# Four chained cross-attention blocks on one core: the second layer's context keys and values are computed at the end of the first joined stage, and one layer norm goes ahead of weight casts

## The chip, the cores and the metric

One Trainium2 chip, one of its cores. The metric is the device time of one launch in microseconds (us). Engines by the names of the profile: PE (TensorE matmul; PEld is its weight load), DVE (VectorE), ACT (ScalarE), POOL (GpSimd), SP (SyncE, which issues all DMAs here).

## The reference, cut to what matters

Tokens x are 2 x 1024 x 256 (B = 2, T = 1024, D = 256); the context is 2 x 77 x 256. Four blocks follow each other. The first two matter here.

```python
# block L0: causal self-attention over the tokens and the context, 16 heads of 16
qkv = _ln(x, g1, be1) @ w_qkv + b_qkv
ckv = context @ w_ckv + b_ckv
k, v = concat([k_self, k_ctx]), concat([v_self, v_ctx])
x = x + softmax(mask(q k^T / 4)) v
hdn = gelu(_ln(_ln(x, g2, be2), gf, bf) @ w1 + b1)        # exact gelu, 1024 wide
x = x + (hdn @ w2 + b2)
# block L1: three layers, 4 heads of 64; the first one attends from the tokens to the context
K = relu(context @ Wk[0] + bk[0]); V = relu(context @ Wv[0] + bv[0])
Q = relu(x @ Wq[0] + bq[0]); out = softmax(Q K^T / 8) V * query_mask + x ; ...
```

K and V of layer 0 of L1 depend on the context and weights alone, not on x. Blocks L2 (cross-attention by token index) and L3 (attention to the context and a feed-forward) are not touched.

## The kernel before, in words

The program is a row of stages. `next_stage` ends each: every engine drains and adds one to a semaphore, and all wait until all five have. POOL then clears the semaphores of the stage that is over. In a stage each engine runs a list of its own, in the order in which it is written; semaphores tie the lists.

**Stage 1, the joined front** (`front_tensor`, `front_scalar`, `front_vector`, `front_gpsimd`, `front_sync`). Normalised tokens are turned, and 18 feature items (L570: queries and keys of L0, 128 features by 512 tokens, split into three bf16 parts by ACT L607 and L588, DVE L642 and POOL L682) alternate with 18 value items (L576, DVE L637). Each item is stored to HBM by SP (L697, L700). The number of a place in this list counts both kinds (0 to 35). From number 24 on, the row maxima of head group 0 run between the items. A maximum is a chunk: PE multiplies into bank 6 or 7 (L1218), DVE reduces it (L1446 or L1450). There are 43 chunks, 7 for context keys and 9 for each of 4 heads. 19 of them and the final M (a transpose of the maxima, L1223, and its split into three bf16 rows, L1465 to L1474) come after the last item. SP loads group 1's stack between the stores (`NEXT_STACK_AT`), and at the end sends the three rows (L1074).

**Stage 2, attention of L0** (`attention_tensor` and others). Eight groups; scores L1251, exponentials ACT L1411, causal triangles POOL L1188, products with values L1276. POOL's list begins with `context_prepare_gpsimd` (L1125, L2065): it clears KBD, the block-diagonal keys of L1's first layer, and writes REP, the context features repeated for four heads. SP loads the feed-forward's weights and L1's first weights and rows in `load_more`.

**Stage 3, feed-forward of L0** (`first_ffn_*`, `ffn_*`). Float weights and tokens are split into a high part and a remainder. Tokens are in four chunks of 512. The list of each engine begins:

- PE: `context_tensor` (L2073 keys, L2082 and L2084 values, six sets of two products and a bias), then the transposes of chunk 0 (L1686), then hidden tiles (L1618, six matmuls each) and, three tiles later, the second product (L1633).
- ACT: high parts of the first half of the weights, roots, chunk 0's normalisation (L1711), `context_keys_scalar` (L2094), `context_values_scalar` (L2102), then chunk 0's two feature tiles (L1678) and their high parts (L1595).
- DVE: moments of chunk 2 (L1767 to L1699), scalings (L1704, L1706), four casts of the second half of the weights (L1786), the scaling of chunk 2, `attention_moments` of chunk 3, the two token remainders of chunk 0 (L1600), without which no hidden tile starts.
- POOL: `split_low` (L1588), four remainders of each half of the weights; then `context_gpsimd` (L2110, L2112), which blanks the foreign heads of the values.

```python
        e.wait_ge(sp.w_high, 1)                       # before, first_ffn_vector
        for i in range(4, 8):
            h = e.tensor_copy(W_H[:, a], W0_FF[:, a])
        scaling(e, n2, 2)
        attention_moments(e, n2, 3)
        for k in range(KT):
            split_tokens_vector(e, s, 0, k)
```

## Time and profile before

| | us |
|---|---|
| three runs | 1535.41, 1539.99, 1544.95 (median 1539.99) |
| the profiled execution, its own time | 1534.61 |
| its span | 1532.9 |
| PE busy | 1328.7 (87%) |
| DVE busy | 1068.3 (70%) |
| ACT busy | 739.0 (48%) |
| POOL busy | 538.3 (35%) |
| stage 1 | about 14 to 93 |
| stage 2 | about 93 to 397.2 |
| stage 3 | from 397.2 |

A busy PE in these rows is not PE at its peak: its matmuls count as busy at either clock, and at the lower one they take longer. PEclk is the granted clock as a share of full speed: 1.00 is 2.4 GHz, 0.50 is 1.2 GHz. The chain of waits is the list of what ended last at each moment; work that is not on it has slack.

### The profile page before, as it was taken

The page shows a single profiled execution, that of the slowest core. Times are in us where ns is not written, and L with a number is a line of the kernel's source. Part 1 is how long each engine was busy: PE and PEld are TensorE (multiplying, and loading weights), DVE is VectorE, ACT ScalarE, POOL GpSimd, SP SyncE. Part 2 cuts the span into 40 slices and gives each one's busy share as a digit, 9 for nine tenths or more (in the row PEclk, how much of TensorE's full clock was granted, in tenths as well). Part 3 has the DMA queues.
Part 4 walks back from the last instruction along what each step waited for, and adds up shares of the span by engine and source line. Part 5 has one row for each costly group of instructions (what it writes and reads, how often), then busy time and mean ns, then how long its engine had stood idle before and what let it go on. Part 6 is the DMA issues. An engine that isn't in the chain of part 4 may idle for free.

```text
span 1532.9 us, 21753 instructions
## 1 busy us (share of the span) xinstructions
PE 1328.7 (87%) x7242; PEld 766.8 (50%) x7242; DVE 1068.3 (70%) x2667; ACT 739.0 (48%) x1030; POOL 538.3 (35%) x462
## 2 busy tenths in 40 slices
PE   7879999998699879879999989799998789688897
PEld 4423333332388656644443356344444577445796
DVE  6668888885654377767566867676777888676654
ACT  4335665667675346423334445233444644344664
POOL 3311111112410053216876622267864356001212
PEclk9969999999899998979999999799999889899998
DMA  6974333300000001562440217704400020630001
GB/s 202 265 197 95 59 59 59 59 2 2 28 1 1 1 1 69 174 177 48 97 97 26 91 52 215 187 15 97 97 28 28 8 29 32 157 66 2 1 1 55
DMA packets 80021, 110.39 MB, mean 72 GB/s; under 512 B 16712, under 2 KB 55810, under 8 KB 78118
## 3 DMA queue, kind: packets, MB, share of 16 engines
q1 hardware_dynamic: 79910, 109.00, 28.5%
q8 instruction: 58, 0.95, 0.3%
q14 instruction: 53, 0.43, 0.1%
HBM read 70.62 MB, written 37.83 MB: 71 GB/s over the span
## 4 chain that ended last, share of the span: by engine, by line
PE 40%; POOLq 19%; DVE 16%; issue 11%; ACT 6%; DVEq 3%; DMA 2%; SPq 1%; POOL 1%; ACTq 0%
POOLq L1165 19%; PE banks L1276 6%; PE banks L1618 5%; PE banks L1633 5%; PE banks L1218 4%; PE banks L2204 3%; PE banks L1251 3%; PE banks L2234 2%; DVE max_parts L1450 1%; DVE mask_rows L1446 1%; PE banks L1229 1%; ACT x_feat L1411 1%; DVE max_parts L1435 1%; PE banks L2222 1%; DVE scratch L1446 1%
## 5 line engine op out<-in xcount | busy, mean ns | idle before, releaser
L1411 ACT ACTIVATE x_feat<-banks,key_bias 128x1024 f32<-128x1024 f32 x160 | 176.4, 1113 | 263.3 <-PE banks L1258 207.1
L1164 POOL TENSOR_TENSOR x_feat<-x_feat 128x1024 f32<-128x1024 f32 (+1 forms) x112 | 243.0, 2170 | 94.4 <-ACT x_feat L1411 85.9
L1218 PE MATMUL banks<-stacks 128*128 128x512 f32 (+4 forms) x640 | 224.2, 399 | 37.1 <-DVE max_parts L1439 12.4
L1276 PE MATMUL banks<-x_feat,v_group 128*32 128x512 f32 (+4 forms) x1312 | 231.6, 569 | 8.4 <-ACT x_feat L1411 4.8
L1411 ACT ACTIVATE x_feat<-banks 128x1024 f32<-128x1024 f32 (+2 forms) x224 | 178.8, 841 | 112.0 <-PE banks L1251 110.9
L1218 PEld LDWEIGHTS banks<-stacks 96*128 96x128 bf16 (+1 forms) x640 | 78.8, 138 | 219.5 <-DVE max_parts L1439 91.8
L1251 PE MATMUL banks<-stacks 99*128 99x512 bf16 (+3 forms) x512 | 129.8, 344 | 18.7 <-ACT x_feat L1411 13.0
L1188 POOL TENSOR_SCALAR_AFFINE_SELECT x_feat<-x_feat 128x256 f32<-128x256 f32 x128 | 53.4, 420 | 244.1 <-ACT x_feat L1411 242.4
L1439 DVE CUSTOM_DVE_ANT_0 scratch<-banks,mask_rows 128x512 f32<-128x512 f32 x128 | 88.2, 689 | 49.8 <-PE banks L1218 49.7
L1257 PE MATMUL banks<-stacks 128*128 128x512 f32 x256 | 110.9, 433 | 9.5 <-DMA stacks<-neg_max_parts_r 9.5
L1618 PE MATMUL banks<-stacks 128*128 128x512 f32 x384 | 102.0, 405 | 9.8 <-DVE stacks L1600 8.9
L1258 PE MATMUL banks<-stacks 96*128 96x512 f32 x256 | 103.2, 403 | 0.0
L1633 PE MATMUL banks<-stacks 128*128 128x256 f32 x768 | 102.9, 286 | 0.0
L1633 PEld LDWEIGHTS banks<-stacks 128*128 128x128 f32 x768 | 99.9, 193 | 3.9
L1450 DVE TENSOR_REDUCE max_parts<-banks 128x1 f32<-128x512 f32 x128 | 84.3, 687 | 13.2 <-PE banks L1218 12.5
L1439 DVE CUSTOM_DVE_ANT_0 w_even<-banks,mask_rows 128x512 f32<-128x512 f32 x112 | 77.0, 688 | 10.8 <-PE banks L1218 10.7
L1618 PEld LDWEIGHTS banks<-stacks 128*128 128x128 f32 x384 | 70.6, 195 | 23.1 <-issue 9.6
L2204 PE MATMUL banks<-x_feat,w_odd 128*128 128x512 f32 x160 | 80.5, 632 | 0.8 <-ACT x_feat L2323 0.8
L1276 PEld LDWEIGHTS banks<-x_feat,v_group 128*32 128x32 f32 (+1 forms) x1312 | 41.5, 119 | 78.5 <-issue 53.1
L1257 PEld LDWEIGHTS banks<-stacks 128*128 128x128 f32 x256 | 49.5, 193 | 60.2 <-issue 42.6
L1251 PEld LDWEIGHTS banks<-stacks 99*128 99x128 bf16 x512 | 44.7, 99 | 56.3 <-ACT x_feat L1411 29.9
L1435 DVE TENSOR_REDUCE max_parts<-banks 128x5 f32<-128x385 f32 (+2 forms) x104 | 53.7, 546 | 27.1 <-PE banks L1207 13.6
(308 smaller groups left out, 2457.4 us busy)
## 6 DMA issues: line engine op xcount, KB each, us to landing
stacks<-q_parts_r SPq DMA_DIRECT2D x18, 512.0 KB, 6.9
stacks<-k_parts_r SPq DMA_DIRECT2D x18, 512.0 KB, 10.5
q_parts_r<-stacks SPq DMA_DIRECT2D x16, 512.0 KB, 3.2
k_parts_r<-stacks SPq DMA_DIRECT2D x16, 512.0 KB, 3.1
v_group<-v SPq DMA_DIRECT2D x14, 512.0 KB, 14.7
stacks<-q_parts SPq DMA_DIRECT2D x16, 384.0 KB, 5.0
stacks<-q_parts SPq DMA_DIRECT2D x16, 256.0 KB, 7.6
w_even<-in_w SPq DMA_DIRECT2D x4, 1024.0 KB, 14.4
```

The costliest lines, as they stand in the source:

```text
L1164: e.tensor_tensor(total, total, p, ALU.add)
L1165: e.drain().then_inc(s.tile_summed, 1)
L1218: m = e.matmul(PS[:, bank, at:at + wide], q[0:rows, h, qt * P:(qt + 1) * P], keys[0:rows, h, k0:k0 + wide], start=True, stop=True, skip_gr ...
L1251: m = e.matmul(o, k[0:rows, head_of_k(A, r, h), k0:k0 + P], q[0:rows, h, qs], start=True, stop=True, skip_group_check=True)
L1257: e.matmul(o, ka[:, hk, ks], qa[:, h, qs], start=True, stop=False)
L1258: m = e.matmul(o, kb[0:96, hk, ks], qb[0:96, h, qs], start=False, stop=True)
L1276: m = e.matmul(PS[w * h:w * (h + 1), bank, t.q0:CH], V[:, h, :], PB[:, t.index % 2, h // 2, h % 2, 0:CH - t.q0], start=t.first, stop=t.las ...
L1411: e.activation(dst, PS[:, 2 * (st % 2):2 * (st % 2) + 2, 0:CH - t.q0], ACT.Exp, scale=A.scale, bias=bias).then_inc(s.p_ready, 1)
L1439: e.tensor_tensor_reduce(scratch, PS[:, bank, :], MB[:, k0:k0 + CH], 1.0, LOWEST, ALU.add, ALU.max, maxp[:, h, qt, half:half + 1]).then_in ...
L1618: mm = e.matmul(PS[:, i % 3, :], w[:, k, ms], x[:, c % 2, k, :], start=k == 0 and w is w1h and x is XH, stop=k == KT - 1 and w is w1l)
L1633: mm = e.matmul(o, h[:, i % 4, ts], w[:, m, :], start=m == 0 and t % 2 == 0 and h is HID_H and w is w2h, stop=m == MT_F - 1 and h is HID_L ...
L2204: m = e.matmul(PS[:, n % 2, :], left, right, start=k == 0, stop=k == KT - 1)
```

## The change

L1's context keys and values leave stages 2 and 3 and go to the end of stage 1. REP is written by POOL ahead of feature item 11 (and lies at another place of the same buffer), KBD is cleared by POOL after the last item. Two weight loads and a row of biases leave `load_more` and go into SP's list after number 22. PE's list at the end of stage 1 first waits until all remainders and values are taken, then runs the 19 chunks with the key products behind chunk 32 and three value sets behind chunks 35, 37 and 39; the other three sets come behind M. ACT's bias and relu and POOL's blanking come at the end of their stage 1 lists, so the barrier waits for them. In stage 3 DVE's four casts go behind chunk 3's moments and chunk 0's token remainders.

```diff
+        for n in "qf":                                   # load_more
+            e.dma_start(W1[0][n], kp(a["W" + n][0])).then_inc(ld.w1a, 16)
-        load_layer(e, 0, ld.w1a)
...
+    REPEAT_AT = 11
+    KEYS_BEHIND, VALUES_BEHIND = 11, {8: (0, 0), 6: (0, 1), 4: (0, 2)}
...
+        need(e, s.left, len(items[0]))                   # front_tensor
+        e.wait_ge(stored0.v_taken, len(items[1]))
         for x in front_maxima(A, len(items[0]), 0):
             attention_chunk(e, A, *x, 0, -1)
+            if x[0] == "A" and len(A.chunks) - x[2] == KEYS_BEHIND:
+                context_keys_tensor(e, cx)
+            if x[0] == "A" and len(A.chunks) - x[2] in VALUES_BEHIND:
+                context_values_tensor(e, cx, *VALUES_BEHIND[len(A.chunks) - x[2]])
+        for j in range(3):
+            context_values_tensor(e, cx, 1, j)
...
+        context_keys_scalar(e, cx)                       # front_scalar, after the last item
+        context_values_scalar(e, cx)
...
+            if i == REPEAT_AT:                           # front_gpsimd
+                e.wait_ge(tn.taken, KT * 3)
+                context_repeat_gpsimd(e)
...
+        e.wait_ge(stored0.v_taken, len(items[1]))
+        e.wait_ge(s.product, len(items[0]))
+        fill(e, KBD, 0.0)
+        e.drain().then_inc(cx.cleared, 1)
+        context_gpsimd(e, cx)
...
+            if number == CONTEXT_WEIGHTS_AT:             # front_sync, 22
+                load_context_weights(e)
...
-        context_tensor(e, cs)                            # first_ffn_tensor
...
-        e.wait_ge(cs.keys_ready, 1)
-        e.wait_ge(cs.values_ready, B)
...
-        context_keys_scalar(e, cs)                       # first_ffn_scalar
-        context_values_scalar(e, cs)
...
+        scaling(e, n2, 2)                                # first_ffn_vector
+        attention_moments(e, n2, 3)
+        for k in range(KT):
+            split_tokens_vector(e, s, 0, k)
         e.wait_ge(sp.w_high, 1)
         for i in range(4, 8):
             a = slice(CH * i, CH * (i + 1))
             h = e.tensor_copy(W_H[:, a], W0_FF[:, a])
         h.then_inc(sp.w_high, 1)
-        scaling(e, n2, 2)
-        attention_moments(e, n2, 3)
-        for k in range(KT):
-            split_tokens_vector(e, s, 0, k)
```

**The first place is PE at the end of stage 1.** Before, from the ninth chunk of head 2 to the second group's first chunk:

```order
L1218 MATMUL banks<-stacks 128x256 x2
L1218 MATMUL banks<-stacks 128x512 x6
L1218 MATMUL banks<-stacks 128x128
L1218 MATMUL banks<-stacks 128x384
L1218 MATMUL banks<-stacks 128x128
L1218 MATMUL banks<-stacks 128x384
L1218 MATMUL banks<-stacks 128x256 x2
L1223 MATMUL banks<-ident,max_rows 32x128
L1251 MATMUL banks<-stacks 128x512 x2
L1207 MATMUL banks<-stacks 128x77 x5
```

Now, from the keys (L2103; w_odd holds Wk and Wv) on. L1254 is the former L1218, L2115 and L2117 are a value set and its bias:

```order
L2103 MATMUL banks<-ctx_feat,w_odd 128x154 x4
L1254 MATMUL banks<-stacks 128x256 x2
L1254 MATMUL banks<-stacks 128x512 x2
L2115 MATMUL banks<-w_odd,w_even 103x128 x2
L2117 MATMUL banks<-rows_odd,ones_row 103x128
L1254 MATMUL banks<-stacks 128x512 x2
L2115 MATMUL banks<-w_odd,w_even 103x128 x2
L2117 MATMUL banks<-rows_odd,ones_row 103x128
L1254 MATMUL banks<-stacks 128x512 x2
L2115 MATMUL banks<-w_odd,w_even 103x128 x2
L2117 MATMUL banks<-rows_odd,ones_row 103x128
```

The keys stand ahead of the last chunk of head 2, the value sets between the chunks of head 3. The rest of the piece, up to the barrier:

```order
L1254 MATMUL banks<-stacks 128x256 x2
L1259 MATMUL banks<-ident,max_rows 32x128
L2115 MATMUL banks<-w_odd,w_even 103x128 x2
L2117 MATMUL banks<-rows_odd,ones_row 103x128
L2115 MATMUL banks<-w_odd,w_even 103x128 x2
L2117 MATMUL banks<-rows_odd,ones_row 103x128
L2115 MATMUL banks<-w_odd,w_even 103x128 x2
L2117 MATMUL banks<-rows_odd,ones_row 103x128
```

Three sets now stand between M and the barrier.

**The second place is DVE at the start of stage 3.** Before, from the second of the first two scalings:

```order
L1706 SCALAR_TENSOR_TENSOR minus_mean_rstd<-mean_var,rstd 128x4
L1786 CAST stacks<-w_even 128x512 x4
L1704 RECIPROCAL rstd<-std 128x4
L1706 SCALAR_TENSOR_TENSOR minus_mean_rstd<-mean_var,rstd 128x4
L1767 TENSOR_TENSOR x_res<-x_res,y_tok 128x1024
L1691 BN_STATS stats<-x_res 128x6 x4
L1696 BN_AGGR mean_var<-stats 128x2 x4
L1699 TENSOR_SCALAR var_eps<-mean_var 128x4
L1600 TENSOR_TENSOR stacks<-x_feat,stacks 128x512 x2
```

Now, the same lines with new numbers:

```order
L1742 SCALAR_TENSOR_TENSOR minus_mean_rstd<-mean_var,rstd 128x4
L1740 RECIPROCAL rstd<-std 128x4
L1742 SCALAR_TENSOR_TENSOR minus_mean_rstd<-mean_var,rstd 128x4
L1798 TENSOR_TENSOR x_res<-x_res,y_tok 128x1024
L1727 BN_STATS stats<-x_res 128x6 x4
L1732 BN_AGGR mean_var<-stats 128x2 x4
L1735 TENSOR_SCALAR var_eps<-mean_var 128x4
L1636 TENSOR_TENSOR stacks<-x_feat,stacks 128x512 x2
L1821 CAST stacks<-w_even 128x512 x4
```

The casts moved behind the two token remainders.

## Rows read from the trace of the kernel before

**Rows 1.** the chain of waits, 70 to 105 us: start us, us, what

```profile
77.85 0.62 PE banks L1218
...
78.50 0.70 DVE max_parts L1450
...
89.00 0.39 PE banks L1223
...
92.29 1.84 DMA stacks<-neg_max_parts
...
94.27 1.02 PE banks L1251 x2
...
100.27 1.72 PE banks L1276 x8
```

**Rows 2.** timeline at full clock: start us, us, engine, line, operation

```profile
77.25 0.39 PE L1218 MATMUL banks<-stacks 96*128 96x512 bf16 x1 [0.21 <-DVE max_parts L1450]
...
133.24 0.60 PE L1251 MATMUL banks<-stacks 99*128 99x512 bf16 x2
```

**Rows 3.** PE by stretch of 1 us: busy (instructions), PEclk, DMA share, GB/s

```profile
75.00:76.00 1.00, 0.00 (x0) 1.00 1.07 329
...
84.00:85.00 1.00, 0.82 (x3) 0.50 0.80 299
...
101.00:102.00 1.00, 1.00 (x11) 0.65 1.19 216
...
408.00:409.00 1.00, 0.63 (x4) 0.95 0.00 0
...
419.00:420.00 1.00, 1.00 (x6) 0.93 0.00 0
```

**Rows 4.** timeline of the work that moves, on PE, ACT and POOL

```profile
95.49 1.34 POOL L2065 COPY w_even<-ctx_feat 128x616 f32<-128x616 f32 x2
...
397.30 1.32 PE L2073 MATMUL banks<-ctx_feat,w_odd 128*128 128x154 f32 x8 [0.89 <-DVEq L279]
...
404.00 0.46 PE L2084 MATMUL banks<-rows_odd,ones_row 1*103 1x128 f32 x2
...
404.78 1.56 ACT L2094 ACTIVATE w_even<-banks,cols 64x154 f32<-64x154 f32 x4
...
406.36 0.87 ACT L2102 ACTIVATE w_even<-banks 103x384 f32<-103x384 f32 x2
...
412.94 0.99 POOL L2110 TENSOR_SCALAR_AFFINE_SELECT w_even<-w_even 103x384 f32<-103x384 f32 x1
...
413.89 0.53 POOL L2112 TENSOR_SCALAR_AFFINE_SELECT w_even<-w_even 103x384 f32<-103x384 f32 x1
```

**Rows 5.** the chain of waits where the joined stage's values end

```profile
74.97 0.33 DVE v_group L637
```

**Rows 6.** timeline of SP: the group 1 values are issued

```profile
82.68 0.34 SPq L1015 DMA_DIRECT2D v_group<-v  x1
```

**Rows 7.** the chain of waits into the feed-forward stage, 385 to 430 us

```profile
404.32 2.08 DVE stacks L1786 x3
...
406.56 1.20 DVE minus_mean_rstd L1706
...
411.27 0.59 DVE stacks L1600
...
411.86 1.68 DVEq L1705
```

**Rows 8.** timeline of POOL, DVE and PE in the feed-forward stage

```profile
400.26 5.19 POOL L1588 TENSOR_TENSOR stacks<-w_even,stacks 128x512 fp32r<-128x512 f32 x4 [5.86 <-ACT stacks L1580]
...
406.48 6.50 POOL L1588 TENSOR_TENSOR stacks<-w_even,stacks 128x512 fp32r<-128x512 f32 x4 [1.03 <-DVE stacks L1786]
...
413.69 0.24 DVE L1706 SCALAR_TENSOR_TENSOR minus_mean_rstd<-mean_var,rstd 128x4 f32<-128x4 f32 x1
...
421.76 1.59 PE L1633 MATMUL banks<-stacks 128*128 128x256 f32 x12
```

More of the change, by code:

```diff
@@ L711, in program, with load_context_weights @@
     NEXT_STACK_AT, FIRST_VALUES_AT = (24, 27, 30), 32
+    CONTEXT_WEIGHTS_AT = 22
+    def load_context_weights(e):
+        for n in "kv":
+            e.dma_start(W1[0][n], kp(a["W" + n][0])).then_inc(cx.loaded, 16)
+        e.dma_start(RB[0:1, 0:1, :], a["rows1"][0:1, :].unsqueeze(0)).then_inc(cx.loaded, 16)
     def front_sync(e, items, A):
@@ L2046, in program @@
     NK = 4 * SC + 1
-    REP = WF[:, 640:640 + KT * B * NK].rearrange("p (k b n) -> p k b n", k=KT, b=B)
+    REP = WF[:, 3584:3584 + KT * B * NK].rearrange("p (k b n) -> p k b n", k=KT, b=B)
     VB = WF[:, 640:640 + 768].rearrange("p (b j n) -> p b j n", b=B, j=3)
@@ L2058, in program, with context_repeat_gpsimd @@
     LSTEPS = 4 * (NC + 2) + 2
-    def context_prepare_gpsimd(e):
-        fill(e, KBD, 0.0)
+    def context_repeat_gpsimd(e):
         fill(e, REP[:, :, :, 4 * SC:NK], 0.0)
@@ L2075, in context_tensor, with context_values_tensor @@
         mm.then_inc(s.key_product, 1)
+    def context_values_tensor(e, s, b, j):
         ones, bias = ONES_ROW[0:1, 0:KROWS], row(RB, ROWS_L1, "bv0")
-        for b in range(B):
-            for j in range(3):
-                cols = slice(64 * j, 64 * j + P)
-                o = PS[0:KROWS, 4 + b, j * P:(j + 1) * P]
-                for k in range(KT):
-                    e.matmul(o, REP[:, k, b, KROWS * j:KROWS * (j + 1)], W1[0]["v"][:, k, cols], start=k == 0, stop=False,
-                             skip_group_check=True)
-                mm = e.matmul(o, ones, bias[0:1, cols], start=False, stop=True, skip_group_check=True)
-        mm.then_inc(s.value_product, 1)
+        if (b, j) == (0, 0):
+            e.wait_ge(s.repeated, 1)
+        cols = slice(64 * j, 64 * j + P)
+        o = PS[0:KROWS, 4 + b, j * P:(j + 1) * P]
+        for k in range(KT):
+            e.matmul(o, REP[:, k, b, KROWS * j:KROWS * (j + 1)], W1[0]["v"][:, k, cols], start=k == 0, stop=False,
+                     skip_group_check=True)
+        mm = e.matmul(o, ones, bias[0:1, cols], start=False, stop=True, skip_group_check=True)
+        if (b, j) == (B - 1, 2):
+            mm.then_inc(s.value_product, 1)
     def context_keys_scalar(e, s):
         e.wait_ge(s.key_product, 1)
+        e.wait_ge(s.cleared, 1)
         for m in range(KT):
@@ L2093, in context_keys_scalar @@
                 at = COLS["L1k"] + m
-                last = e.activation(KBD[rows, m, :, SC * h:SC * (h + 1)],
+                e.activation(KBD[rows, m, :, SC * h:SC * (h + 1)],
                                     PS[rows, m, 0:B * SC].rearrange("p (b n) -> p b n", b=B), ACT.Relu, bias=COL[rows, at:at + 1])
-        last.then_inc(s.keys_ready, 1)
     def context_values_scalar(e, s):
@@ L3169, in _ @@
         e.wait_ge(ld.w1c, 32)
+        e.wait_ge(ld.w1a, 48)
         nxt()
```

32 lines of the change are left out of this document (17 added, 15 removed).

## The prediction, before the changed kernel ran

> **What bounds the kernel now.** I read the chain of waits first, because each of the changed places lies at a seam between two stages, where busy shares say little. At the end of stage 1 it alternates between a chunk on PE, 0.62 us, and its maximum on DVE, 0.70 us; after the transpose of the maxima it runs through the three row transfers, which land at 94.13, to PE's first scores at 94.27 [rows 1]. The timeline shows the same chunk in 0.39 us, and a pair of score products in 0.60 instead of 1.02, where the clock is full [rows 2]. So I read the granted clock next: PE did nothing from 75 to 76, and the clock was half while PE's records filled 0.8 of each microsecond; it was full again only within 101 to 102 [rows 3]. It fell again at 408.95, after PE had stood idle but for one set of transposes since 405.6, and came back at 419.07, 5.4 us after PE had begun to work without a gap [rows 3]. Last I read the timeline of the work that moves [rows 4] and the chain into the feed-forward [rows 7], where DVE and not the moved work is what ends last.
>
> **Stage 1, the added wait.** PE may start chunk 24 only when the last value is taken, at 75.30 [rows 5]; before, that chunk was ready and DVE took it at once. One chunk of 0.39 [rows 2] and some 0.25 of semaphores and fill are now waited for: +0.7. Behind the wait stand only the 19 chunks. Below it can't go much, as the wait is certain; above it could be 0.9, if the clock has already fallen.
>
> **Stage 1, the inserts.** The key products took 1.32 us; the six value sets filled 398.6 to 404.46, so 1.0 each, all at full clock [rows 4]. At half clock I stretch them by 1.6, the ratio of the chunk (0.62 to 0.39): 2.1 and 1.6. DVE needs 1.39 for two chunks, and at half clock PE's 0.62, DVE's 0.70 and 0.07 between them are 1.39 too [rows 1]: no slack, so an insert costs its length less 0.1, and the keys 0.2 less again, since the chunk ahead of them takes DVE longer. That is 1.8 + 3 x 1.5 = 6.3. At full clock the same circle takes 1.16, which leaves 0.23 ahead of time and 0.3 in the chunk behind: keys 0.6, sets 0.5, together 2.1. The upper bound is the doubling of the full-clock prices, 8.1.
>
> Between 2.1 and 6.3 the clock decides. Work at 0.8 of the records did not bring it back in eleven microseconds; work without a gap did, after 3.3 us up to 101.35 and after 5.4 us up to 419.07 [rows 3]. With the inserts PE has hardly a gap from the keys on. I take it that the clock comes back behind the first value set: 1.8 + 1.5 + 2 x 0.5 = 4.3. The Trainium skill (TensorE: Matmul & The Clock Gate, "What's actually happening") says that the array is throttled by default and that sustained activity releases it. By that rule the sum is the one with 4.3; by the rows from 78 to 88 alone, where a busy PE stayed slow, it is the one with 6.3.
>
> **Stage 1, the tail.** M's transpose ends at 89.39 [rows 1]. Behind it come three sets (3.0 at full clock, 4.8 at half), ACT's two activations (0.87), POOL's two blankings (0.99 and 0.53 beside DVE work; DVE is idle here, so 0.53 each) [rows 4], and 0.4 of semaphores and drains: PE could start at 94.7 or 96.5. It started at 94.27, for the rows landed then. So +0.4 or +2.2; with doubled sets +3.5. SP's loads of group 2 start as much later; nothing asks for them in the first tiles. The split of the maxima and the row transfers run beside this and are covered.
>
> **Stage 1, what is covered.** REP's two copies (1.34 [rows 4]) stand ahead of item 11 on POOL, which idled 34 us in this stage waiting for ACT; if that cover were gone, item 11's store would be 1.7 late, and its buffer is asked for by nobody after it. Two weight loads of 256 KB and a row enter SP's queue at about 54 us, ahead of the stores and of group 1's stack. At the 267 GB/s of those microseconds they cost the queue 2 us. The group 1 values are issued at 82.68, when all stores have landed [rows 6]; 2 us later is still ahead of 89, so 0. If a store's landing did hold a buffer, the whole 2 us would be paid.
>
> **Stage 2.** POOL's preparation at 94.5 to 96.8 [rows 4] was over before the first triangle at 99.9: its removal is worth 0. With the clock full at the start, the six PE pieces of the chain from 94.27 to 101.98 (the first 1.02, the last 1.72 [rows 1], 5.3 in all) shrink to 0.6 of it: -2.1. If the clock is half, 0.
>
> **Stage 3.** PE's context products (397.30 to 404.46) ended before the first transposes could start at 404.93: 0. ACT's six activations (1.56 + 0.87 [rows 4]) delayed chunk 0's feature tiles by 1.6, but DVE reached their remainders only at 411.19: off the path. What lies on it is DVE's list [rows 7]: the casts, 2.08, leave it. The scaling's 1.20 stays, since POOL still works on the first half until 405.45 [rows 8]. The second remainder shows 1.68 for a piece that should be about 0.7, beside POOL's second half (406.48 to 412.98 [rows 8]); now POOL waits for the casts at that time and is idle: -0.9. Together -3.0, and the first hidden tile starts at 410.7 instead of 413.68. ACT's high part of the second tile, freed of the six activations, is ready at 408.7, in time.
>
> The price is POOL's second half. It starts at 413.0, behind the casts (410.5 + 2.5), and takes 5.19 to 6.50 [rows 8]: it ends at 418.2 to 419.5. The second product, at 421.76 before [rows 8], now asks for it at 418.7. So the gain is 2.2 to 3.0; I take 3.0. A DVE operation on 4 columns took 1.20 beside POOL's subtraction [rows 7] and 0.24 once it was over [rows 8]. The Trainium skill (SBUF — State Buffer, "Who interferes with whom") says why: a VectorE instruction with two SBUF inputs and a GpSimd instruction that reads SBUF block each other whole. By that rule the first three remainders of the hidden tiles may each wait for one of POOL's four pieces, and these for them; the trace agrees with the rule, and what it can cost is rival 3.
>
> **The sum.** 0.7 + 4.3 + 0.4 - 2.1 - 3.0 = +0.3. The profiled execution took 1534.61, which is 5.4 under the median of the three runs; the forecast is 1534.9 for such an execution and 1540.3 for the median.
>
> **The rivals.**
> 1. *The clock stays at half to the end of stage 1.* For it: it did so for eleven microseconds before [rows 3], and the waiting for the last value makes the gap ahead longer. Against it: the inserts fill the gaps. 0.7 + 6.3 + 2.2 - 3.0 = +6.2, so 1546.2; slower than before. With all upper bounds 0.7 + 8.1 + 3.5 - 2.2 = +10.1. It decides if the granted clock is still 0.50 when M is transposed. 30%.
> 2. *The clock never falls, or is back with the keys.* 0.7 + 2.1 + 0.4 - 2.1 - 3.0 = -1.9, so 1538.1. For it only that PE's gaps are what let it fall, and the keys come 5 us after. 12%.
> 3. *The change doesn't do what it says in stage 3*: POOL's second half becomes the new end. If its four pieces and three DVE remainders of 0.7 take turns, it ends at 421.5, and nothing is gained there: 0.7 + 4.3 + 0.4 - 2.1 = +3.3, so 1543.3. 10%.
> 4. *The weights push a store past its buffer's turn*: +2 on the forecast, 1542.3. Against it: 7 us between the issue of the group 1 values and their use. 6%.
>
> **How the numbers follow.** The forecast has 42%. About 1%, 15 us, is what a measurement of this kernel can tell from no change, and no case reaches it. The three runs lie within 9.5 us, so half of that, 4.8, goes on either side: from 1538.1 - 4.8 = 1533 to 1546.2 + 4.8 = 1551, and one more for the upper bounds. Faster by over 1% 2%, within 1% 94%, slower by over 1% 4%, all for what no case has priced.
>
> **What would show it.** Right: DVE's idle time between 76 and the barrier grows by 4 to 6 us, with the clock back at 1.00 before M; the first scores some 5.5 us later than 94.27; stage 2 shorter by 2; from the barrier of stage 3 to the first hidden tile 13.4 us instead of 16.4, with the casts behind it. Wrong: a clock of 0.50 at the start of stage 2, a hidden tile that waits for ACT or for POOL, or a store that ACT waits for.

## The result and the profile after

| | kernel before | changed kernel |
|---|---|---|
| median of the runs (range) | 1536.54 us (1530.77 to 1544.95, 12) | 1541.01 us (1535.44 to 1552.2, 12) |
| ratio, 95% interval | | 1.0039 [1.0023, 1.0056] |
| profiled execution, own time / span | 1534.61 / 1532.9 | 1545.09 / 1543.3 |

The change makes the kernel slower by 0.39%: 6.0 us, between 3.5 and 8.6. The forecast was +0.3, which lies outside that interval. That the forecast time, 1540.3, lies 0.7 from the new median is mostly luck: the three runs that it started from had their median 3.5 above that of the twelve.

I read each stage as the time between the moments at which the last engine is through `next_stage` (us, one profiled execution each, one row for each kernel). Read so, stage 1 of the kernel before runs from 5.9 to 93.3, not from about 14:

| kernel | load | stage 1 | stage 2 | stage 3 | stage 4 | span |
|---|---|---|---|---|---|---|
| before | 5.9 | 87.4 | 304.0 | 119.3 | 163.6 | 1532.9 |
| changed | 6.1 | 93.5 | 305.9 | 115.4 | 161.4 | 1543.3 |
| e11, the changed kernel again | 6.6 | 99.0 | 308.4 | 116.0 | 159.8 | 1543.1 |
| e1 casts only | 6.2 | 86.7 | 303.9 | 116.5 | 159.3 | 1528.5 |
| e2 context only | 7.0 | 92.0 | 305.4 | 118.6 | 162.2 | 1538.3 |
| e3 all sets ahead of M | 6.6 | 91.0 | 305.4 | 115.9 | 159.7 | 1532.9 |
| e4 = e1 + idle products behind M | 6.7 | 87.5 | 303.9 | 116.5 | 159.3 | 1529.9 |
| e5 context beside | 6.6 | 87.7 | 305.6 | 114.9 | 159.3 | 1526.9 |
| e6 late wait | 6.6 | 95.4 | 306.9 | 115.4 | 162.2 | 1539.7 |
| e7 idle products, late | 6.6 | 102.3 | 304.3 | 115.1 | 162.1 | 1544.4 |
| e8 = e5 + idle products in stage 3 | 6.4 | 86.4 | 304.4 | 114.7 | 161.5 | 1530.6 |
| e9 = e8 + idle products from 72 us | 6.0 | 85.4 | 304.0 | 122.0 | 161.0 | 1530.9 |
| e10 = changed + idle products from 72 us | 6.5 | 89.0 | 304.0 | 115.5 | 160.9 | 1534.1 |
| e12 = changed, PE's code shifted | 6.6 | 95.5 | 302.8 | 115.9 | 157.6 | 1533.5 |

Stage 4's code is the same everywhere, and it varies between 157.6 and 163.6: so much of a span's difference means nothing. In the first three stages the changed kernel stands at +6.1, +2.0 and -3.9, together +4.2, which is within the interval of the runs; the rest of the 10.4 between the two spans lies almost wholly in stages whose code is the same.

The timeline of the changed kernel where stage 1 ends (start us, us, engine, line, operation, in brackets the idle time ahead and what ended it; line numbers are up to 36 higher than before):

```profile
75.16 0.41 DVE L655 TENSOR_TENSOR v_group<-banks,rows_even 128x256 f32<-128x256 f32 x1
75.67 0.59 PE L1254 MATMUL banks<-stacks 96*128 96x256 bf16 x3 [2.38 <-DVE v_group L655]
76.09 0.42 DVE L1482 CUSTOM_DVE_ANT_0 w_even<-banks,mask_rows 128x256 f32<-128x256 f32 x1 [0.52 <-PE banks L1254]
...
81.33 2.26 PE L2103 MATMUL banks<-ctx_feat,w_odd 128*128 128x154 f32 x8
...
84.06 0.42 DVE L1482 CUSTOM_DVE_ANT_0 w_even<-banks,mask_rows 128x256 f32<-128x256 f32 x1 [1.67 <-PE banks L1254]
...
85.12 0.60 PE L2115 MATMUL banks<-w_odd,w_even 128*103 128x128 f32 x4
...
92.05 0.37 PE L1259 MATMUL banks<-ident,max_rows 128*32 128x128 f32 x1 [1.43 <-DVE max_rows L1491]
...
92.22 1.06 PE L2115 MATMUL banks<-w_odd,w_even 128*103 128x128 f32 x4
...
97.56 0.87 ACT L2136 ACTIVATE w_even<-banks 103x384 f32<-103x384 f32 x2 [12.36 <-PE banks L2117]
...
99.66 1.04 PE L1287 MATMUL banks<-stacks 99*128 99x512 bf16 x2 [2.13 <-POOLq L284]
```

PE waits 2.38 for the last value, and DVE 0.52 for the chunk behind it. The keys take 2.26 at half clock and leave DVE idle for 1.67. The first value set is at full clock (0.60 for its four products), the first one behind M at half (1.06). The first scores now start when the barrier lets them (released by POOL), at 99.66; before they waited for the rows until 94.27 [rows 1].

The changed kernel by stretches of 1 us (PE, PEld, DVE, ACT, POOL busy and instructions; PEclk, DMA share, GB/s):

```profile
84.00:85.00 1.00, 0.55 (x3) 0.11 (x2) 0.94 (x5) 0.96 (x4) 0.00 (x0) 0.77 0.48 86
85.00:86.00 1.00, 1.00 (x7) 0.71 (x6) 1.00 (x3) 0.20 (x1) 0.00 (x0) 1.00 0.81 262
...
91.00:92.00 1.00, 0.00 (x0) 0.00 (x0) 0.80 (x5) 0.00 (x0) 0.00 (x0) 0.64 0.00 0
92.00:93.00 1.00, 0.95 (x5) 0.92 (x5) 0.48 (x2) 0.00 (x0) 0.00 (x0) 0.50 0.00 0
...
108.00:109.00 1.00, 1.00 (x11) 0.62 (x9) 0.80 (x2) 0.41 (x1) 0.00 (x0) 0.83 1.07 184
```

The clock came back behind the keys, a set sooner than forecast. It fell again while PE waited 1.43 us for the last maximum, and stayed at half through the late sets, the barrier and the first nine microseconds of stage 2.

The timeline of the changed kernel in stage 3, whose barrier opens at 405.5 (before: 397.3):

```profile
408.56 4.93 POOL L1624 TENSOR_TENSOR stacks<-w_even,stacks 128x512 fp32r<-128x512 f32 x4 [5.87 <-ACT stacks L1616]
...
413.31 1.09 PE L1722 MATMUL banks<-ident,y_tok 128*128 128x128 f32 x4 [8.61 <-ACT y_tok L1747]
...
417.95 0.69 DVE L1636 TENSOR_TENSOR stacks<-x_feat,stacks 128x512 fp32r<-128x512 f32 x1 [0.55 <-ACT stacks L1631]
418.56 1.43 DVE L1821 CAST stacks<-w_even 128x512 fp32r<-128x512 f32 x4
...
418.79 7.38 PE L1654 MATMUL banks<-stacks 128*128 128x512 f32 x24 [2.35 <-DVE stacks L1636]
420.07 5.47 POOL L1624 TENSOR_TENSOR stacks<-w_even,stacks 128x512 fp32r<-128x512 f32 x4 [6.59 <-DVE stacks L1821]
420.15 1.22 DVE L1742 SCALAR_TENSOR_TENSOR minus_mean_rstd<-mean_var,rstd 128x4 f32<-128x4 f32 x1
...
426.00 1.24 PE L1669 MATMUL banks<-stacks 128*128 128x256 f32 x9
```

The remainders of the tokens come ahead of the casts. The first hidden tile starts 13.2 us behind the barrier (16.4 before), the second product 20.5 behind it (24.5 before [rows 8]). All four casts take 1.43 with POOL idle, where the list before needed 2.08 for three of them, about half of that beside POOL's first half, which ends at 405.45 [rows 7, 8].

### The profile page after: what moved, and what is told of

It reads as the page before. It is cut to its first block, busy times and chain, and to the rows that moved or that the text cites. A ratio compares the mean times of both kernels' runs of the same rounds, so it can differ in the third digit from the quotient of the medians.

```text
span 1543.3 us, 21761 instructions
## 1 busy us (share of the span) xinstructions
PE 1331.5 (86%) x7242; PEld 772.4 (50%) x7242; DVE 1072.3 (69%) x2667; ACT 738.8 (48%) x1030; POOL 536.7 (35%) x462
## 4 chain that ended last, share of the span: by engine, by line
PE 40%; POOLq 20%; DVE 14%; issue 13%; ACT 7%; DVEq 3%; DMA 2%; SPq 1%; POOL 1%; ACTq 0%
POOLq L1201 19%; PE banks L1312 5%; PE banks L1654 5%; PE banks L1669 5%; PE banks L1254 4%; PE banks L1287 3%; PE banks L2238 3%; PE banks L2268 2%; ACT x_feat L1447 1%; DVE mask_rows L1482 1%; PE banks L2786 1%; PE banks L1265 1%; PE banks L578 1%; DVE max_parts L1486 1%; PE banks L2256 1%
## 5 line engine op out<-in xcount | busy, mean ns | idle before, releaser
L1254 PE MATMUL banks<-stacks 128*128 128x512 f32 (+4 forms) x640 | 222.7, 397 | 40.7 <-DVE max_parts L1475 14.5
L1447 ACT ACTIVATE x_feat<-banks 128x1024 f32<-128x1024 f32 (+2 forms) x224 | 178.9, 841 | 114.9 <-PE banks L1287 113.7
L1254 PEld LDWEIGHTS banks<-stacks 96*128 96x128 bf16 (+1 forms) x640 | 79.2, 139 | 219.9 <-DVE max_parts L1475 93.3
L2238 PE MATMUL banks<-x_feat,w_odd 128*128 128x512 f32 x160 | 76.4, 604 | 0.8 <-ACT x_feat L2357 0.8
L1471 DVE TENSOR_REDUCE max_parts<-banks 128x5 f32<-128x385 f32 (+2 forms) x104 | 53.7, 546 | 30.8 <-PE banks L1243 16.4
```

The costliest lines, as they stand in the source:

```text
L1254: m = e.matmul(PS[:, bank, at:at + wide], q[0:rows, h, qt * P:(qt + 1) * P], keys[0:rows, h, k0:k0 + wide], start=True, stop=True, skip_gr ...
L1447: e.activation(dst, PS[:, 2 * (st % 2):2 * (st % 2) + 2, 0:CH - t.q0], ACT.Exp, scale=A.scale, bias=bias).then_inc(s.p_ready, 1)
L2238: m = e.matmul(PS[:, n % 2, :], left, right, start=k == 0, stop=k == KT - 1)
```

## The experiments

### Which half of the change costs

e1 is the kernel before with the reordering of stage 3 alone, e2 the changed kernel with the old order of stage 3:

```diff
 # e1, first_ffn_vector of the kernel before (e2 does the reverse in the changed kernel)
+        scaling(e, n2, 2)
+        attention_moments(e, n2, 3)
+        for k in range(KT):
+            split_tokens_vector(e, s, 0, k)
         e.wait_ge(sp.w_high, 1)
...
         h.then_inc(sp.w_high, 1)
-        scaling(e, n2, 2)
-        attention_moments(e, n2, 3)
-        for k in range(KT):
-            split_tokens_vector(e, s, 0, k)
```

> The kernel before with one part of the change: DVE's four casts go behind chunk 3's moments and the two token remainders of the feed-forward stage; the context work stays where it was. Theory A (the reordering makes the whole gain of that stage, the moved context work none): from the stage's barrier to the first hidden tile 13.5 to 14 us instead of 16.4, since only the second remainder now waits 0.6 for ACT, the stage 3 to 4 us shorter than 119.3, first stages unchanged, in all -3 to -4 us against before, ratio 0.9975. Theory B (the gain came from PE and ACT being freed of the context products and activations): the first hidden tile 15.5 to 16.4 us behind the barrier, ratio 1.000.

> The changed kernel with the casts put back ahead of chunk 3's moments: only the context work is moved. Theory A: first stage 6 us longer than before (93.5 for 87.4), second stage 0 to 2 longer by the clock at its start, third stage within 0.5 of before, in all +6 to +8 us, ratio 1.0045. Theory B: third stage 3 us shorter than before, in all +4, ratio 1.0026.

e1: 1529.73 against 1535.28, ratio 0.9969 [0.9957, 0.9982]. e2: 1541.54, ratio 1.0046 [1.0027, 1.0065]. So the reordering gains some 4.8 us and is faster than either kernel; the move of the context costs about 7. In e2 stage 3 is 0.7 shorter and its first hidden tile starts 16.4 behind the barrier, as before: moving the context's work out of stage 3 is worth almost nothing by itself. With the reordering it is worth more, since ACT's six activations then stand in the way, as e1's timeline shows:

```profile
407.75 1.09 PE L1686 MATMUL banks<-ident,y_tok 128*128 128x128 f32 x4 [2.48 <-ACT x_feat L1678]
...
411.19 7.58 PE L1618 MATMUL banks<-stacks 128*128 128x512 f32 x24 [2.35 <-DVE stacks L1600]
...
418.60 1.59 PE L1633 MATMUL banks<-stacks 128*128 128x256 f32 x12
```

The second transposes wait 2.48 for ACT. Behind the barrier (396.8) the hidden tile starts at 14.4 and the second product at 21.8, 1.1 and 1.3 later than in the changed kernel.

### The late sets

```diff
-    KEYS_BEHIND, VALUES_BEHIND = 11, {8: (0, 0), 6: (0, 1), 4: (0, 2)}
+    KEYS_BEHIND, VALUES_BEHIND = 11, {9: (0, 0), 8: (0, 1), 7: (0, 2), 6: (1, 0), 5: (1, 1), 4: (1, 2)}
-        for j in range(3):
-            context_values_tensor(e, cx, 1, j)
```

> The changed kernel with all six value sets between the last chunks, none behind the transpose of the maxima. Theory A (three sets behind the transpose at half clock, then ACT and POOL, hold the barrier): barrier at once behind the row transfers, so the first scores 4.9 us behind the transpose instead of 7.6; the three sets cost 0.5 each among the chunks at full clock and 1.7 each at half, so the first stage is 1 us shorter (full clock) or 2 us longer (half clock) than the changed kernel's. Taken: 1 us shorter, ratio 1.003 against before. Theory B (the tail is set by ACT and POOL, whatever PE does): the scores still 7 us behind the transpose, ratio 1.004 to 1.005.

```profile
93.47 0.27 PE L1257 MATMUL banks<-ident,max_rows 128*32 128x128 f32 x1 [1.42 <-DVE max_rows L1489]
98.66 1.01 PE L1285 MATMUL banks<-stacks 99*128 99x512 bf16 x2 [4.92 <-DMA stacks<-neg_max_parts]
```

M comes 1.4 later than in the changed kernel, but the first scores again wait for the rows, 5.2 behind M, and start 1.0 sooner; stage 1 is 91.0 (93.5), in part because 0.98 of the wait for the rows now falls behind the barrier. The work behind M was no free filler: at half clock, with ACT's and POOL's part behind it, it outlasts the transfer that was to cover it. The runs don't resolve this: ratio 1.0046 [1.0029, 1.0063].

### The clock behind M

e4 is e1 with eight idle products of PE (bf16, 512 columns, read by nobody) behind M:

```diff
+        e.wait_ge(s.left, len(items[0]))
+        for _ in range(8):
+            e.matmul(PS[:, 0, :], IDB[:, :], CAUSAL, start=True, stop=True)
```

> The kernel before with the casts moved (as in the first run) and eight bf16 products of 128 by 512 on PE behind the transpose of the maxima, whose result nobody reads; they fill 3.4 us at half clock of the 4.9 in which PE waits. Theory A (a half clock at the start of the second stage costs up to 2 us): the clock is back at 1.00 within 2 us of the first scores instead of 7, and the second stage is 1.5 to 2 us shorter than 303.9; in all -5 against before, ratio 0.9965. Theory B (ACT and DVE set the pace there, the clock costs nothing): the second stage as in the first run, ratio as the first run's; if the barrier is held, worse.

```profile
90.09 3.62 PE L585 MATMUL banks<-mask_rows,ident_bf 128*128 128x512 bf16 x8
```

```profile
91.00:92.00 1.00, 1.00 (x4) 0.40 (x3) 0.68 (x3) 0.00 (x0) 0.00 (x0) 0.50 0.00 0
...
101.00:102.00 1.00, 1.00 (x8) 0.23 (x9) 0.56 (x1) 0.95 (x1) 0.27 (x1) 0.50 0.87 186
```

3.62 us without a gap did not bring the clock back. Stage 2 took 303.9. Ratio 0.9974 [0.9959, 0.9989], as e1.

e7 is the changed kernel with such products (128 columns, bank 2): 8 behind each of four maxima and 24 behind the last set. The 24 that were meant to stand ahead of M are not in the kernel: the last maximum is marked "L" and not "A", so that the condition for them never holds, and the trace has 56 such products in stage 1, not 80. PE still stands idle for 1.31 us ahead of M.

```diff
                 context_values_tensor(e, cx, *VALUES_BEHIND[len(A.chunks) - x[2]])
+            if x[0] == "A" and len(A.chunks) - x[2] in (7, 5, 3, 2):
+                idle_products(e, 8)
+            if x[0] == "A" and len(A.chunks) - x[2] == 1:
+                idle_products(e, 24)
         for j in range(3):
             context_values_tensor(e, cx, 1, j)
+        idle_products(e, 24)
```

> The changed kernel with idle 128-column bf16 products of TensorE into bank 2, whose result nobody reads: 8 behind each of four of the last seven maxima, 24 ahead of M's transpose, 24 behind the last value set. Theory (the prediction's tail and stage 2 failed because the clock fell again at 91.3 us, when TensorE waited 1.4 us for the last maximum; held at full, the three late value sets take 1.06 each, not 1.79, and stage 2 starts at full clock): M still at about 92, first scores 5.6 to 6.0 us behind M (7.6 changed, 5.3 before), stage 1 at 91.2 to 92.0 (93.5), stage 2 at 301.5 to 302.5 (305.9 changed, 304.0 before), so 5 us off the changed kernel and about equal to the kernel before minus 2. Rival (the clock falls at this place whatever TensorE does, as the 3.62 us of idle products in e4 did not bring it back): granted clock 0.50 from 91 to 108, stage 1 at 93.5 or more, stage 2 at 305 to 306.

```profile
84.00:85.00 1.00, 1.00 (x5) 1.00 (x5) 0.99 (x6) 0.00 (x0) 0.00 (x0) 0.50 0.07 22
...
98.00:99.00 1.00, 1.00 (x10) 0.95 (x9) 0.71 (x4) 0.00 (x0) 0.00 (x0) 0.50 0.00 0
```

The rival's mark came true, and more: the clock didn't come back behind the keys either, though PE's records fill every microsecond from 88 to 99. So e7 shows nothing of what a filled gap ahead of M is worth at full clock. The idle products, doubled in length, stand in stage 1's 102.3. Ratio 1.0019 [0.9998, 1.004].

### Is it an accident of the execution?

e11 is the changed kernel itself, profiled once more.

> The changed kernel itself once more, for the clock at the end of stage 1. Theory (whether TensorE's clock comes back behind the context's keys is an accident of the execution, as it did in three profiles with the keys there and did not in the two of the last study): either low from 77 to 84 and again from 91 to 108 with stage 1 at 93 to 94, or low from 77 to over 105 with stage 1 at 95 to 96. Rival (it is a matter of the kernel's own order of instructions, and the late wait changed it): stage 1 at 93.5 and the clock as in the first profile of this kernel, within 0.5 us.

```profile
92.00:94.00 2.00, 2.00 (x8) 1.27 (x7) 1.29 (x3) 0.00 (x0) 0.00 (x0) 0.50 0.00 0
```

```profile
97.96 0.37 PE L1259 MATMUL banks<-ident,max_rows 128*32 128x128 f32 x1 [1.31 <-DVE max_rows L1491]
```

It is. The same program was at half clock from 77.4 to 114.9 without a break, M came 5.9 later than in its first profile (2.2 of that had been lost by the last value, behind another fall at 50.1), and stage 1 took 99.0. Of the seven profiles with keys in stage 1 and no idle products shortly ahead of them, the clock returned about the end of the keys in three (changed, e2, e3) and not in four (e6, e7, e11, e12).

### The added wait

e6 moves the two waits from ahead of maximum 24 to ahead of the keys.

```diff
-        need(e, s.left, len(items[0]))
-        e.wait_ge(stored0.v_taken, len(items[1]))
         for x in front_maxima(A, len(items[0]), 0):
             attention_chunk(e, A, *x, 0, -1)
             if x[0] == "A" and len(A.chunks) - x[2] == KEYS_BEHIND:
+                need(e, s.left, len(items[0]))
+                e.wait_ge(stored0.v_taken, len(items[1]))
                 context_keys_tensor(e, cx)
```

> The changed kernel with TensorE's two added waits (all features left, all values taken) moved from ahead of maximum 24 to just ahead of the context's keys. Theory (the wait costs what VectorE's 25th maximum is late, 0.5 to 0.6 us, and nothing else): the maxima run 0.5 to 0.6 us sooner, M is transposed about 0.5 sooner, stage 1 is 93.0 us (93.5 in the changed kernel), everything behind it unchanged. Rival (it cost more, since it also delays when the inserts fall against the clock): stage 1 at 92 or less. Rival (the time goes into the next wait, keys against values taken): stage 1 at 93.5.

```profile
75.34 0.41 DVE L1482 CUSTOM_DVE_ANT_0 w_even<-banks,mask_rows 128x256 f32<-128x256 f32 x1
```

The maximum follows the last value by 0.33 from start to start (75.01 to 75.34), and by 0.93 in the changed kernel (75.16 to 76.09): the wait costs 0.6. The rest was the clock again (half from 77.5 to 111.6; stage 1 95.4), so the stage's length says nothing here. Ratio 1.0021 [0.9996, 1.0046].

### Holding the clock before it falls

e9 is e8 (below) and e10 the changed kernel, both with idle products from 72 us on:

```diff
+        idle_products(e, 20)              # 128 columns, bank 3
         for x in front_maxima(A, len(items[0]), 0):
+            if x[0] == "M":
+                idle_products(e, 20)
             attention_chunk(e, A, *x, 0, -1)
+            if x[0] == "A":                      # e10: where no insert stands
+                idle_products(e, 4)
+        idle_products(e, 16, CH)          # 512 columns; e10: 7, behind the late sets
```

> e8 with idle bf16 products of TensorE into bank 3 through the end of stage 1 as well: 20 of 128 columns where TensorE waits 1.29 us at 74.7 us, 4 behind each of the last maxima (the 0.2 us that it waits for VectorE there), 20 ahead of M's transpose, 16 of 512 columns behind it (3.4 us at full clock). Nothing of the context is moved. Theory (the clock falls at 77.8 us because TensorE waits so long before it; kept busy from 74.7 on it stays at full speed): no 0.50 from 77 to 101, maxima still paced by VectorE, stage 1 at 87.0 to 87.5 us (87.4 before), stage 2 at 301.9 to 302.4 (304.0 before), which is the prediction's stage 2 term by itself; stage 3 at 114.7; ratio to before 0.9945 to 0.9965. Rival (the clock falls anyway): the idle products double in length, the last ones end at or behind the barrier, stage 1 at 88 to 90, stage 2 at 304 to 305.5.

> The changed kernel with such idle products from 74.7 us on: 20 ahead of the added wait, 4 behind each of the last maxima that carry no insert, 20 ahead of M's transpose, 7 of 512 columns behind the last value set. Theory (the prediction's failed step is the clock alone): at full clock throughout, keys 1.3 us and value sets 1.06 each between the maxima, M transposed at about 91.0 (92.05 in the changed kernel, 89.00 before), first scores 5.7 behind it (7.6; 5.3), stage 1 at 90.3 to 91.3 (93.5), stage 2 at 301.9 to 302.5 (305.9), stage 3 at 115.4. Rival (the clock falls anyway): stage 1 at 95 to 98, stage 2 at 305 to 307.

The timeline of e9:

```profile
87.20 0.27 PE L1234 MATMUL banks<-ident,max_rows 128*32 128x128 f32 x1 [0.30 <-DVE max_rows L1466]
...
92.38 0.59 PE L1262 MATMUL banks<-stacks 99*128 99x512 bf16 x2 [1.46 <-DMA stacks<-neg_max_parts]
...
95.43 0.61 PE L1262 MATMUL banks<-stacks 99*128 99x512 bf16 x2 [1.67 <-ACT x_feat L1422]
...
116.88 0.60 PE L1240 MATMUL banks<-ident,o_feat 128*128 128x128 f32 x4
```

And of e10:

```profile
90.28 0.27 PE L1270 MATMUL banks<-ident,max_rows 128*32 128x128 f32 x1 [0.30 <-DVE max_rows L1502]
...
95.51 0.61 PE L1298 MATMUL banks<-stacks 99*128 99x512 bf16 x2 [0.52 <-POOLq L284]
```

Here the clock stayed full until 96.5 and 98.2. (The last maximum has no products behind it but the 20 ahead of M.) With it held, the move's own price can be read from e10 against e9. From the start of the last value to M it is 15.34 against 12.95: 2.39, of which the wait is 0.6 and the inserts 1.8. From M to the first scores it is 5.23 against 5.18. Held clock also gains: from the last value to M e9 takes 12.95 against 14.11 before. That is 1.2 of the 2.0 by which its stage 1 is under the kernel before; the rest is within what stage 1 varies by, 86.4 to 87.7, in the four profiles in which its code is that of before (before, e1, e5, e8). But stage 2 is 304.0 in both, as before, although it began at full clock (for 4 and 3 us behind the first scores). e9's first round ends (the transposes of its sums, 116.88) 24.5 behind the first scores, against 24.9 before (119.18 - 94.27): behind the first tiles PE waits 1.67 for ACT. In e10 it is 25.3, in the changed kernel 25.5 and in e12 (below), at half clock for the first seven microseconds, 24.7: the round's length doesn't follow the clock. The runs give e9 0.9946 [0.9918, 0.9974] and e10 0.9951 [0.993, 0.9971]: the changed kernel with its clock held is faster than the kernel before. The table's sum for e10, -2.2 in stages 1 to 3, is smaller than the runs say, -7.5 (-4.5 to -10.8). The profile is of a long execution, 1535.82, where e10's median is 1530.86.

e9's profile shows what holding can't guard: a fall at 393.5, ahead of stage 3, where the context's work still stands.

```profile
395.41 2.42 PE L2087 MATMUL banks<-ctx_feat,w_odd 128*128 128x154 f32 x8 [0.90 <-DVEq L279]
...
408.22 1.11 PE L1697 MATMUL banks<-ident,y_tok 128*128 128x128 f32 x4
```

The transposes start 12.8 behind the keys' start (7.6 in e8), and stage 3 took 122.0.

### Why stage 2 is longer

The first round of stage 2 ends 25.5 behind the barrier in the changed kernel and 25.9 in the one before. The stage's loss comes later, in the same code. Each round ends with the transposes of its sums; these are round 5's and 6's in the changed kernel:

```profile
201.58 0.60 PE L1265 MATMUL banks<-ident,o_feat 128*128 128x128 f32 x4
...
221.58 0.60 PE L1265 MATMUL banks<-ident,o_feat 128*128 128x128 f32 x4
```

They are 20.0 apart, in the kernel before 19.4 (195.60 to 215.04); rounds 8 and 10 take 0.5 and 0.3 more. Who waited for the negated maxima in stage 2 behind its first ten microseconds (us in total, times), in the kernel before:

```profile
  PE banks L1251: 0.5, 1
...
DMA to landing us min/median/max: 1.7/1.8/2.1
```

and in the changed kernel:

```profile
  PE banks L1287: 1.2, 3
...
DMA to landing us min/median/max: 1.7/1.9/3.3
```

The second kernel's PE waits for three of them instead of one, since in four of the seven transfers of three rows one lands 2.6 to 3.3 us behind its issue. There a 16 KB packet of the instruction queue (58 packets, 0.95 MB in the page) starts 1.6 to 2.5 us behind the issue of the first of the three; in the kernel before none starts within 2 us ahead and 6 us behind. The DMA view of the changed kernel from 216 to 218 us (packets, MB, share; issues, KB each, median us to landing) shows the packet beside two of the transfers:

```profile
q8 instruction: 1, 0.02, 3.0%
...
stacks<-neg_max_parts SPq DMA_DIRECT2D x2, 8.0 KB, 2.7
```

and that of the kernel before from 210 to 212, in the same round, has none:

```profile
stacks<-neg_max_parts SPq DMA_DIRECT2D x2, 8.0 KB, 1.9
```

This holds across all fourteen profiles: of their 98 transfers of three rows, 19 have such a packet 1.6 to 2.6 us behind the first issue, and these 19 alone have a landing of 2.6 us or more; packets from 2.8 us on or ahead of the issue delay none. e12 shifts PE's code and leaves the rest of the work as it is:

```diff
         turn_ctx_tensor(e, tnc, CTXN)
+        for _ in range(32):
+            e.matmul(PS[:, 3, 0:P], IDB[:, :], CAUSAL[:, 0:P], start=True, stop=True, skip_group_check=True)
```

> The changed kernel with 32 idle 128-column bf16 products of TensorE right behind the context's first transposes, in a gap of 3.98 us in which TensorE waits for VectorE (2.1 us of products at full clock): nothing else moves, but every later instruction of TensorE stands 64 instructions further down its program, so that its code is fetched at other moments. Theory (stage 2 is not longer for its clock at the start, since its first round ends 25.5 us behind the barrier against 25.9 in the kernel before; it is longer because the 16 KB packets of the instruction queue start 1.6 to 2.5 us behind the issue of the negated maxima in four of seven rounds, and these then land up to 3.3 us behind their issue instead of 2.1): the fetches come some 4.6 us sooner against the rounds, no landing of the negated maxima over 2.3 us behind stage 2's first round, stage 2 at 303.9 to 304.5 us (305.9 changed, 308.4 in its second profile), or up to 1.3 more if the 3.4 us at half clock near the stage's end fall inside a round; stages 1 and 3 as in the changed kernel (93 to 99, 115.4 to 116). Rival (the late landings come from the context's buffers or weights being where they are): landings over 3.0 us in three or more rounds again, stage 2 at 305.4 or more.

```profile
  PE banks L1289: 0.5, 1
...
DMA to landing us min/median/max: 1.8/1.9/2.2
```

The same packets now start between 0.9 us ahead of the first issue and 0.1 behind it. The late landings are gone, the rounds of 19.4 take 19.4 or 19.5 again, and stage 2 is 302.8, the shortest of all, with the clock at half until 109 in its first seven microseconds. Ratio 1.0008 [0.9986, 1.003] against 1.0039 for the changed kernel. The maximum was over 3.2 in all five profiles with the context in stage 1 and no idle products (changed, e2, e3, e6, e11) and at most 2.2 in the other nine. e7, e10 and e12 are among these, which have the context in stage 1 and more idle products: what counts is not the context's work itself but how many PE instructions stand ahead. A second part of stage 2's loss is a fall of the clock for 3.4 us at 371.2 inside round 14 (21.8 instead of 20.6); before it fell at 378.2, behind that round's end. The clock falls near this place in every one of the fourteen profiles, somewhere between 362 and 392. In e5, whose stage 2 is that of the kernel before, it fell from 362.2 to 369.0, and round 14 took 22.3: this is why e5's stage 2 is 305.6 without a late landing. So this part isn't shown to be the move's.

### A version that keeps the gain

e5 is e1 with the context left in stage 3 but off ACT's path: keys in banks 6 and 7, the six activations behind chunk 0's tokens.

```diff
# context_tensor and context_keys_scalar: PS[:, m, ...] becomes PS[:, 6 + m, ...]
# first_ffn_scalar
-        context_keys_scalar(e, cs)
-        context_values_scalar(e, cs)
         for k in range(KT):
             take_alone(e, tn, 0, k, 3, cols)
             split_tokens_scalar(e, s, tn, 0, k)
+        context_keys_scalar(e, cs)
+        context_values_scalar(e, cs)
# first_ffn_tensor
-        e.wait_ge(cs.keys_ready, 1)
-        e.wait_ge(cs.values_ready, B)
         def between(c, m):
+            if (c, m) == (0, 2):
+                e.wait_ge(cs.keys_ready, 1)
+                e.wait_ge(cs.values_ready, B)
```

> The kernel before with the stage 3 reordering of e1 (DVE's four casts behind chunk 3's moments), and the context's work left in stage 3 but off ScalarE's way to the first hidden product: keys go to banks 6 and 7, and ScalarE copies and splits chunk 0's tokens before it takes the context's keys and values. Theory (the second transposes wait 2.48 us for ScalarE's copy in e1, and that copy stands behind the context's 2.43 us of activations): the second transposes come 2.0 to 2.4 us sooner, the first hidden product 13.0 to 13.5 us behind the stage's barrier (14.4 in e1, 13.3 in the changed kernel), the second product about 20.6 behind it (21.8 in e1, 20.5 changed), stage 3 at 115.0 to 115.6 us (116.5 in e1, 119.3 before), stage 1 as before (87.4). So the changed kernel's gain in stage 3 without its cost in stage 1: ratio to before 0.9960 to 0.9975. Rival (the first gelu is late instead, since ScalarE's context activations now stand ahead of it, and the second product is bound by GpSimd's second half anyway): second product at 21.5 or later, stage 3 at 116.3 to 117.

```profile
412.50 7.75 PE L1618 MATMUL banks<-stacks 128*128 128x512 f32 x24 [2.70 <-DVE stacks L1600]
...
420.09 1.60 PE L1633 MATMUL banks<-stacks 128*128 128x256 f32 x12
```

The second transposes wait 0.96 for ACT instead of 2.48. Stage 3 is 114.9, shorter than in the changed kernel, and the second product starts 20.2 behind the barrier (399.9). Nothing had to go to stage 1. Ratio 0.9966 [0.9951, 0.9981].

e8 adds idle products between chunk 0's transposes.

```diff
         for k in range(KT):
             turn_one(0, k)
+            for _ in range((6, 8)[k]):
+                e.matmul(PS[:, 2, :], IDB[:, :], CAUSAL, start=True, stop=True)
```

> e5 with idle 512-column bf16 products into bank 2 between chunk 0's transposes in stage 3: 6 behind the first four transposes, 8 behind the second four (1.3 and 1.7 us at full clock). Theory (the clock falls there because TensorE waits 2.4 us twice): no fall at 405 us, the second transposes take 0.65 instead of 1.09, the first hidden products 0.2 us less each: stage 3 at 114 to 114.7, about 1 us under e5. Rival (the time is set by ScalarE's copies and GpSimd's second half, not by TensorE): the clock stays full and stage 3 is within 0.4 us of e5. Rival (the clock falls anyway, with idle products at half speed ahead of the transposes): stage 3 0.5 to 1.5 us above e5.

```profile
404.00:406.00 2.00, 1.49 (x9) 0.99 (x10) 1.93 (x3) 1.25 (x3) 1.15 (x1) 1.00 0.01 4
...
410.00:412.00 2.00, 2.00 (x10) 1.64 (x10) 1.58 (x6) 1.93 (x5) 0.89 (x1) 1.00 0.00 0
```

```profile
416.73 1.66 PE L1633 MATMUL banks<-stacks 128*128 128x256 f32 x12 [1.03 <-POOL stacks L1588]
```

The clock never fell there, and stage 3 is 114.7, 0.2 under e5: the first rival was right, PE's clock is not what this seam costs. The hidden tile starts 12.6 behind the barrier in both; in e8 the hidden tiles are done sooner, and the second product then waits 1.03 for POOL's second half, so that it starts only 0.7 sooner than in e5. Ratio 0.9956 [0.9935, 0.9978], not to be told from e5. e1, e4, e5, e8, e9 and e10 all beat both kernels by intervals that overlap, by 0.3% to 0.5% against the kernel before; e5 does it with no idle work.

## Why the prediction was right in level and wrong in its sum

- **The wait, +0.7**: 0.6 (e6). Right.
- **The inserts, +4.3** (2.1 at full clock, 6.3 at half). From the last value's start to M: 16.89 in the changed kernel against 14.11 before; without the wait 2.2. In e10 1.8 at full clock, in e11 5.9, in e12 5.7 and in e6, which has no wait there, 5.4 at half. Both ends were priced well, and the clock came back one set sooner than taken, in that execution. That it may not come back at all is the other half of the term.
- **The tail, +0.4**, with +2.2 at half clock. Measured: M to first scores 7.61 against 5.27, +2.3. This is the first step that failed. The prediction let the clock stay full once it was back; the stretches show that it fell at 91.3, while PE stood 1.43 us without work ahead of M. e10, with the clock held, has +0.05.
- **Stage 2, -2.1**: +2.0 from barrier to barrier; from the first scores on, as the prediction counts it, +2.9, since the scores no longer wait 0.97 for the rows behind the barrier. The second step that failed, in two ways. Its condition, full clock at the start, was not met; it is the prediction's own sign of being wrong ("a clock of 0.50 at the start of stage 2"). And in e9 and e10, where it was met for 4 and 3 us, the first round was 0.4 shorter and 0.4 longer than before. The six pieces summed from the chain [rows 1] are on it only until ACT's exponentials set the pace, 3 us behind the first scores. The loss is neither of these. 1.3 of it are late landings beside code loads (rounds 6, 8 and 10; e12 has none), 1.2 a fall of the clock in round 14, of which e5 has 1.7 without the move, and 0.6 the first round, which e12 doesn't have at the same clock; its cause stays open.
- **Stage 3, -3.0**: -3.9 and -3.3 in the two profiles of the changed kernel. Right in mechanism. "Off the path" was wrong for ACT's activations once the order is changed: e1 alone gives -2.7, and e5 1.6 more. The price that was named, POOL's second half, was not paid: it ends at 425.5, and PE goes from the hidden tiles to the second product at 426.00 without a wait. It is paid only where the hidden tiles are faster (1.03 in e8). The Trainium skill (SBUF — State Buffer, "Who interferes with whom") says that VectorE instructions with two SBUF inputs and GpSimd's reads block each other. The trace agrees again: the 4-column scaling takes 1.22 beside POOL's second half, 0.24 alone [rows 8]. But it didn't make a new end here (rival 3).
- **The sum.** Up to the first scores the prediction has +5.4, and measured is +5.4 (94.27 to 99.66; 5.1 in these three terms, 0.3 ahead of them), a coincidence of 2.1 too much in the inserts and 1.9 too little in the tail. The whole is 0.6 + 2.2 + 2.3 + 2.9 - 3.9 = +4.1 in the first profile, where the forecast was +0.3. The largest error is stage 2's, 5.0.
- **Rival 1** had its mark, granted clock 0.50 when M is transposed, in both profiles, and its price, +6.2, is close to the measured difference, +6.0. That closeness is luck too, since it has no loss in stage 2. In the first profile the way was another (back, then down again) and the terms add up to +4.1; in e11 the way was the one described, and they add up to 0.6 + 5.9 + 2.3 + 5.4 - 3.3 = +10.9. It deserved more than the forecast. Rivals 2 and 4 didn't happen: the group 1 values were issued 1.0 later, hidden. (The 267 GB/s of rival 4's price are the mean from 60 to 80 us, not the rate at 54.)

On the rule that sustained activity releases the clock (the Trainium skill, TensorE: Matmul & The Clock Gate, "What's actually happening"): the rows of e4 and e7 speak against counting on it within one seam. PE's records were full for 3.6 us and from 88 to 99, and the clock stayed at half.

## What to carry to other kernels

The worth of inserts on PE hung on a clock that the same program has in one execution and hasn't in another: price both, profile the kernel twice, and be wary of putting work that streams at PE's clock where PE has idled before. Ask first whether the work is in anybody's way where it stands: here the gain of a move across stages was had by reordering two lists (e5). A term for a faster start holds only until the next engine's pace takes over. When a filler is placed by a condition, count its instructions in the trace (e7). And when identical code takes longer in one kernel than in another, look for the instruction queue's packets beside the short DMAs that are waited for.

## What the runs showed of the hardware

- Held from before its fall, the granted clock stayed at 1.00 with PE idle for up to 1.7 us at a time (e9, e10); once it was at 0.50, full PE records for 11 us didn't raise it (e7), and it was back within 1 us of the end of the keys, 2.1 to 2.3 us of float products, in three profiles out of seven.
- A 16 KB code packet that started 1.6 to 2.6 us behind the issue of the first of three 8 KB row transfers went with a landing of 2.6 to 3.6 us for one of them, instead of about 1.9 (19 of 98 in fourteen profiles). 64 more instructions in PE's program moved the packets away, and the late landings were gone (e12).
- Casts of 128x512 from f32 to fp32r took 0.36 each with POOL idle; a DVE operation on 4 columns took 1.22 beside POOL's subtraction and 0.24 alone.
